# TensorE's order in a slot of a mixture-of-experts stage: the fourth first product moves between the two second blocks, the fold moves next to them, the output product moves further ahead

## The reference

```python
h = x @ Wm + bm
t = h.reshape(bs * L_ * H, HD)            # 8 heads of 32 values for each of 6272 tokens
logits = t @ expert_emb                   # 16 experts
w = jax.nn.softmax(logits, axis=-1)
topw, topi = jax.lax.top_k(w, K)          # K = 2
hmid = gelu(einsum('td,edi->tei', t, W1) + b1)      # 32 -> 128, every expert
eo = einsum('tei,eio->teo', hmid, W2) + b2          # 128 -> 32
comb = (take(eo, topi) * topw).sum(axis=1)
out = comb.reshape(bs, L_, d) @ Wo + bo
```

## Time and profile before

| what | us |
|---|---|
| median of three executions | 2507.97 |
| span of the profiled execution, first to last instruction | 2591.8 |
| first gelu starts at | 1591.31 |
| last gelu starts at | 2579.26 |
| TensorE busy over the span | 2121.8 |
| ScalarE busy over the span | 1290.9 |
| VectorE busy over the span | 1395.6 |
| mean granted TensorE clock | 0.881 of full |

### The profile page before, as it was taken

The page is one execution under the profiler, slowest core; times in us unless marked ns, Lnnn a source line. Parts: engine busy times, 40 slices in busy tenths (PEclk is TensorE's granted clock), DMA queues, the critical chain, the costliest instruction groups (busy, mean ns, idle before and its releaser), DMA issues. The chain is left out here.

```text
span 2591.8 us, 36453 instructions
## 1 busy us (share of the span) xinstructions
PE 2121.8 (82%) x12850; PEld 1177.0 (45%) x12851; DVE 1395.6 (54%) x2117; ACT 1290.9 (50%) x1634; POOL 955.1 (37%) x673
## 2 busy tenths in 40 slices
PE   6998699997966727783788953989898999999998
PEld 3444355554544525662455631444343443434344
DVE  5666345544576721221456635575666667575843
ACT  3444122223542301111334423878787888887887
POOL 4332211110025750005444002555554655555554
PEclk7999689997976659996688976999999999999999
DMA  2100221216143415553122123555464655555554
GB/s 51 32 26 7 84 63 60 68 35 215 54 131 112 128 59 154 172 173 100 56 75 78 44 68 88 141 138 151 120 171 123 155 139 148 146 145 139 141 140 110
DMA packets 206933, 274.84 MB, mean 106 GB/s; under 512 B 49190, under 2 KB 163446, under 8 KB 206646
## 3 DMA queue, kind: packets, MB, share of 16 engines
q1 hardware_dynamic: 173366, 227.84, 32.2%
q0 software_dynamic: 12288, 25.72, 3.3%
q10 hardware_dynamic: 21120, 19.18, 2.2%
HBM read 203.76 MB, written 68.83 MB: 105 GB/s over the span
## 5 line engine op out<-in xcount | busy, mean ns | idle before, releaser
L2269 ACT ACTIVATE BIG<-psA,b_s 128x1024 f32<-128x1024 f32 x784 | 810.8, 1114 | 225.5 <-PE psA L2213 225.5
L2213 PE MATMUL psA<-x_r,w_r 128*128 128x512 f32 x1568 | 484.6, 432 | 47.6 <-ACT BIG L2269 28.1
L2202 POOL TENSOR_TENSOR BIG<-BIG 128x1024 f32<-128x1024 f32 x147 | 367.5, 2500 | 384.5 <-DVE BIG L2290 190.2
L2290 DVE SCALAR_TENSOR_TENSOR BIG<-psY,b_s,BIG 128x512 f32<-128x512 f32 x392 | 289.5, 748 | 302.9 <-PE psY L2223 294.3
L2213 PEld LDWEIGHTS psA<-x_r,w_r 128*128 128x128 f32 x1568 | 274.6, 193 | 313.5 <-ACT BIG L2269 225.1
L2223 PE MATMUL psY<-BIG,w_s 128*32 128x512 f32 x3136 | 397.7, 622 | 7.7 <-DVE BIG L2306 6.2
L2223 PEld LDWEIGHTS psY<-BIG,w_s 128*32 128x32 f32 x3136 | 82.6, 112 | 214.5 <-issue 134.7
L1174 POOL DMA_INDIRECT xg_d<-xnb,SLOT x128 | 135.1, 1056 | 112.5 <-issue 78.2
L1608 POOL DMA_INDIRECT gath<-yg_d,SLOT x128 | 124.2, 970 | 121.2 <-DVE yn L1617 84.0
L715 DVE TENSOR_REDUCE b_nm<-psN 112x32 f32<-112x512 f32 x128 | 83.1, 686 | 152.8 <-PE psN L612 152.3
L1507 PE MATMUL ps<-BIG,xv 128*128 x528 | 132.5, 394 | 39.3 <-ACT xv L1518 28.5
(11 more groups left out here) (379 smaller groups left out, 3345.4 us busy)
## 6 DMA issues: line engine op xcount, KB each, us to landing
BIG<-wt_d SPq DMA_DIRECT2D x784, 128.0 KB, 2.8
xv<-hs_d SPq DMA_DIRECT2D x196, 128.0 KB, 3.1
BIG<-ypad_d SPq DMA_DIRECT2D x144, 120.0 KB
xg_d<-ex SPq DMA_DIRECT2D x64, 264.0 KB, 3.8
xv<-xg_d SPq DMA_DIRECT2D x66, 256.0 KB, 3.0
xv<-x SPq DMA_DIRECT2D x64, 196.0 KB, 2.7
yg_d<-ex ACTq DMA_DIRECT2D x33, 256.0 KB, 3.3
yg_d<-sq ACTq DMA_DIRECT2D x33, 256.0 KB, 3.3
```

The lines of the kernel that those rows point to most:

```text
L2202: eng.tensor_tensor(gacc[:, w % 2], gacc[:, w % 2], gsum[:, a % 2], ALU.add).then_inc(Q["acc"], 1)
L2213: mm = eng.matmul(psA[m % 3][:, b * BLK:(b + 1) * BLK], w1_r[:, m % 16], x_r[:, w % 2, b * BLK:(b + 1) * BLK], start=True, stop=True)
L2269: eng.activation(hid[:, m % 8], psA[m % 3][:], ACT.Gelu, bias=b1_s[:, m % 16:m % 16 + 1]).then_inc(Q["gel"], 1)
L2290: eng.scalar_tensor_tensor(out=dst, in0=psY[use % 2][:], scalar=b2_s[:, g % 4:g % 4 + 1], in1=wb[:, g % 3, b * BLK:(b + 1) * BLK], op0=ALU ...
```

## The change

Three things move. In TensorE's slot, block 0 now stands after the third first product and block 1 after the fourth, where both stood after the third. The fold stands right before block 0, where it stood after the first of the four first products. The output product and the transposes stand after the second first product, where they stood after the first one. The numbering of psY's uses and VectorE's order follow: last and transposes come ahead of the fold. No slot has both last and fold, so that this matters only where transposes and fold meet.

```diff
-            EXTRAS[k] = [kind for kind, table in (("fold", FOLD), ("last", LAST), ("route", ROUTE)) if k in table]
+            EXTRAS[k] = [kind for kind, table in (("last", LAST), ("route", ROUTE), ("fold", FOLD)) if k in table]
@@ TensorE
                     for e in range(4):
                         if k < NG:
                             first(4 * k + e)
-                        if e == 0 and "fold" in EXTRAS[k]:
+                        if e == 1 and "last" in EXTRAS[k]:
+                            last(*LAST[k], EXTRA_USE["last", k])
+                        if e == 1 and "route" in EXTRAS[k]:
+                            route_pe(eng, ROUTE[k], EXTRA_USE["route", k])
+                        if e == 2 and "fold" in EXTRAS[k]:
                             fold(FOLD[k], EXTRA_USE["fold", k])
-                        if e == 0 and "last" in EXTRAS[k]:
-                            last(*LAST[k], EXTRA_USE["last", k])
-                        if e == 0 and "route" in EXTRAS[k]:
-                            route_pe(eng, ROUTE[k], EXTRA_USE["route", k])
-                        if e == 2 and 0 < k <= NG:
-                            for b in range(NB):
-                                second(k - 1, b)
+                        if e >= 2 and 0 < k <= NG:
+                            second(k - 1, e - 2)
@@ VectorE
                 for k in range(SLOTS):
-                    if "fold" in EXTRAS[k]:
-                        combine(FOLD[k], EXTRA_USE["fold", k])
                     if "last" in EXTRAS[k]:
                         finish(*LAST[k], EXTRA_USE["last", k])
                     if "route" in EXTRAS[k]:
                         route_copy(eng, ROUTE[k], EXTRA_USE["route", k])
+                    if "fold" in EXTRAS[k]:
+                        combine(FOLD[k], EXTRA_USE["fold", k])
```

## The result

The changed kernel takes 2522.74 us (median of 8 runs, 2516.39 to 2530.91) against 2506.47 of before in the same comparison. The ratio is 1.0067, 95% interval 1.0047 to 1.0087: slower by 12 to 22 us. The forecast was a rise of 9 us, to 2517; the rise is 16 us. It had the direction, and the measured time lies in the range. The likeliest class had been "within half a per cent", the median is just past it.

The account below looks back on a forecast made before the run. No engine was near full; ScalarE's gelus waited on TensorE's first products, with VectorE the chain in places of router segments. Terms -0.9 + 6.3 + 3.7 + 0.7 + 0.3 - 0.9 = +9.2 us on 2508 gave 2517, range 2497 to 2535.

Parts of the forecast that it names:

- The likeliest class: Whole kernel: time the same within half a per cent, 12.5 us; chance 0.50, against slower 0.36 and faster 0.14.
- The step on plain slots: Plain slots: TensorE's pieces with their joints sum to 4.26 us against 4.46, -0.20, where the removed wait seems worth 0.44.
- the rows of single blocks: Trace rows pricing TensorE's joints: a single block with a first product behind it takes 1.00 us, a pair of blocks 1.86.
- Outside the segments and at the end: Plain, F and L slots outside router segments: -7.8 + 0.6 + 6.3 = -0.9 us; last gelu at the end: -0.9.
- The step on VectorE's chain: Weighing of slot 92 to transposes: VectorE busy 9.57 us, unchanged, so the plain slot before the transposes gains nothing.
- its own terms, 9.92 and 6.39: TensorE before the transposes: 9.92 us from block 1 of slot 92, holding 6.39 of work, so a pause of some 3.4.
- The work behind the transposes: R slots, transposes to block 1: 3.09 us against 2.32, +0.77 in each of 14 R slots.
- The segments of the second kind: 7 router segments begun in an R slot, where VectorE has room: 0.53 us each, 3.7, and 0.7 for two.
- the segments of the first kind: 7 router segments begun behind a pause, VectorE the chain in three slots: 0.90 us each, 6.3 in all.
- the rival of the moved collision: Router steps 13 and 14: new spacing frees one from running beside GpSimd, 14 R slots start 2.0 earlier, 2489; chance 0.06.
- the rival of the growing clock: R slots: longer pause before the transposes brings the low clock everywhere, +15 us on the forecast, 2532; chance 0.28.

Follow-up runs that it names:

- the single moves: Against the kernel before, one move each: only blocks parted, ratio 1.0128; only the fold moved, 1.0042; only output product and transposes moved, 0.995.
- the early steps: Changed kernel with router steps of r = 2 and more one slot earlier against their transposes: 2461.70 us, ratio 0.9825 against the kernel before.

## Why the prediction was right and where it was short

The step on plain slots was right: 4.26 forecast, 4.24 measured, and the wait for the fourth first product gave 0.22 where 0.44 seemed to be there, because the new joints cost as the rows of single blocks said. The formula of the Trainium skill ("TensorE: Matmul & The Clock Gate", Back-to-back issue gap), which has no joint, would have put the slot at ScalarE's pace; the trace does not. F slots were forecast at 4.72 and took 4.68, L slots 5.11 and took 5.11 (medians outside the segments). Outside the segments and at the end -1.8 was forecast, and -2.9 measured.

The step on VectorE's chain was right: 8.81 against 8.82 us from weighing to transposes, in most R slots whatever TensorE's order, in the change and in the single moves. The pause is 3.49; the forecast says some 3.4, though its own terms, 9.92 and 6.39, give 3.53. The work behind the transposes, priced at 3.09, is 3.02 in the R slots of the early steps, 0.70 more than the 2.31 of the order of before there; the change itself has no R slot at the full clock to show it. The experiments with earlier steps show it from the other side.

The sum was short. For segments, R slots and slots 0 to 5 the terms give 11.0, the trace 16.6. So the rise of 16 us where 9 was forecast is a matter of size, and two terms were too small:

- The segments of the second kind. I gave VectorE room there and booked -0.37 for two plain slots and the F slot. The plain slots did gain 0.22 each, but in 3 of 7 the F slot behind them rose from 4.69 to 5.5 or 5.6, in 3 others by 0.1: +2.9 us. The first L slots of 2 of these segments rose by 0.7 each, where 0.33 was booked. The timeline of slots 97 and 98 shows why:

```profile
2005.60 2.38 DVE L2046 TENSOR_TENSOR rt<-rt,rs 98x512 f32<-98x512 f32 x1
...
2009.05 2.39 POOL L2188 TENSOR_TENSOR x_r<-xv,x_r 64x1024 fp32r<-64x1024 f32 x1
...
2009.60 2.39 DVE L2050 SCALAR_TENSOR_TENSOR rt<-rt 98x512 f32<-98x512 f32 x1
...
2012.47 1.06 PE L2223 MATMUL psY<-BIG,w_s 128*32 128x512 f32 x8 [0.86 <-DVE ex L2298]
```

  and the same step in the kernel before:

```profile
2084.67 0.69 DVE L2050 SCALAR_TENSOR_TENSOR rt<-rt 98x512 f32<-98x512 f32 x1
```

  Step 7 takes 2.39 because GpSimd splits the next input at that moment. Two things bring them together. In all 7 segments the parted blocks put step 7 from 0.5 us ahead of the first gelu of the F slot to 0.9 behind it. And the split, which waits for its input, starts 0.3 to 0.4 behind that gelu in the 3 bad segments, where step 7 takes 2.3 to 2.4; in the other 4 the input comes 2 us later, the split starts 1.8 to 2.5 behind the gelu, and step 7 takes 0.7 to 1.6. Why the input comes earlier in those 3 is not shown. In the segments of the first kind the F slot rose too, from 5.06 to 5.54; there it gives back most of the 0.66 that three plain slots gained, and the term came out as forecast. This is the rival of the moved collision, with the other sign.
- The clock, which the forecast left as it was. R slots grew by 16.5 us in 14 slots, of which 13.6 is work by the prices (0.77 and the 0.20 that the plain slot in front handed on), or 12.6 with the 0.70 of the early steps. The 2.9 to 3.9 left are the half-clock stretches, which now meet every R slot. This was the rival of the growing clock; it came true at a fifth to a quarter of its price. Taking the mean R slot less its form at the full clock, the clock costs 1.2 us with a pause of mostly 2.08, 2.0 with mostly 2.72 and, with the forms worked out from the prices, 2.2 with 3.49 and 2.4 with 3.96.

A part is open: the medians differ by 16.3 us, the profiled stages by 13.6; 2.7 us are inside the interval. And what in the single case decides how long the clock stays low is not shown: pauses of 3.48 and 3.50 gave R slots of 10.14 and 11.21.

## What to carry to other kernels

Before a wait is taken away by another order on an engine, price that order with the joints that it adds, each from a row where such pieces already meet; a wait of 0.33 us per slot had only 0.22 to give, and the full slots paid 0.33. An order that puts work behind a wait for another engine's chain pays it after the wait, at whatever clock the pause leaves. Here the chain itself was the thing to move: router steps one slot earlier in the order of before gave 2461.6 us, a ratio of 0.982, and the changed order of TensorE then took the same time. An order for one kind of slot has to be priced with its neighbours: parted in plain slots alone, the blocks cost the F slots behind them more than they gave.

## What the runs showed of the hardware

With a pause of TensorE of 2.07 to 2.48 us in front of the transposes 4 of 14 R slots ran at the full 2.4 GHz, with 2.38 to 3.00 (blocks parted in plain slots alone) 3, with 2.71 to 3.41 (the kernel before) 2, and with 3.2 and more in all of them (four runs) none. With no pause (steps one slot earlier) all 14 did. An elementwise VectorE step on 98x512 with two operands in SBUF takes 0.69 us alone and 2.3 to 2.76 when it runs beside a GpSimd operation of 2.4 us from start to end; a reduction of the same size stayed at 0.69 (in the kernel before, under a GpSimd operation from 2030.08 to 2032.46). A block of column-tiled products costs 0.86 us behind another one and 1.00 with a first product behind it.
